# Attention units with score rounds by key tile, one value product for two heads and two query sets, and row sums added by GpSimd

## The reference

```python
def layer(x, q_w, k_w, v_w, o_w, q_b, k_b, v_b, o_b, w_gate_up, w_down):   # x: 2 x 1024 x 512
    x = x + layernorm(attn(layernorm(x)))
    x = x + layernorm(ffn(layernorm(x)))
    return x

def attn(h):                       # 16 heads of 32
    q, k, v = h @ q_w.T + q_b, h @ k_w.T + k_b, h @ v_w.T + v_b
    scores = einsum('bhqd,bhkd->bhqk', q, k) / sqrt(32)
    scores = where(ki > qi, -inf, scores)          # causal
    return einsum('bhqk,bhkd->bhqd', softmax(scores), v) @ o_w.T + o_b

def ffn(h):                        # 512 -> 2 x 2048 -> 512
    gate, up = split(h @ w_gate_up.T)
    return (silu(gate) * up) @ w_down.T
```

## Time and profile before

| | |
|---|---|
| Median of three runs (lowest, highest) | 1198.62 us (1198.29, 1202.72) |
| Span of the profiled execution | 1201.2 us; the page gives no time around it |
| Mean granted TensorE clock | 0.975 of full speed |
| Busy over the span: PE, DVE, ACT, POOL | 95%, 61%, 37%, 29% |
| Chain that ended last | PE 84%, DVE 10% |
| First T, first output matmul of batch 1 | 85.5 us, 599.1 us |

### The profile page before, as it was taken

The page is one execution under the profiler, slowest core; times in us unless marked ns, Lnnn a source line. Parts: engine busy times, 40 slices in busy tenths (PEclk is TensorE's granted clock), DMA queues, the critical chain, the costliest instruction groups (busy, mean ns, idle before and its releaser), DMA issues.

```text
span 1201.2 us, 17984 instructions
## 1 busy us (share of the span) xinstructions
PE 1137.4 (95%) x5888; PEld 784.8 (65%) x5888; DVE 729.2 (61%) x1431; ACT 446.7 (37%) x811; POOL 350.0 (29%) x205
## 2 busy tenths in 40 slices
PE   3889999999999999999997999989999899989996
PEld 2664555555575555554476888878888688868885
DVE  6674667677777766677586454564446454564444
ACT  3214555555414555555523222322223222232221
POOL 5000000000422000003044544534544444534541
PEclk9988999999999999999897999999999999999999
DMA  5312222222312222222223222243233332243230
GB/s 201 88 44 59 59 69 61 61 61 64 94 62 72 63 62 61 61 61 53 80 88 123 81 103 102 82 149 104 79 105 114 116 102 102 81 149 105 79 122 36
DMA packets 51305, 103.85 MB, mean 86 GB/s; under 512 B 9792, under 2 KB 9792, under 8 KB 51008
## 3 DMA queue, kind: packets, MB, share of 16 engines
q1 hardware_dynamic: 51264, 103.33, 28.0%
HBM read 69.74 MB, written 8.39 MB: 65 GB/s over the span
## 4 chain that ended last, share of the span: by engine, by line
PE 84%; DVE 10%; issue 2%; DMA 1%; ACT 1%; SPq 1%; POOL 0%; DVEq 0%; POOLq 0%; ACTq 0%
PE ps L975 18%; PE ps L977 17%; PE ps L976 17%; PE ps L1072 13%; PE ps L1055 10%; PE ps L1029 6%; PE ps L1058 2%; PE ps L1040 1%; DVE outs_sums L737 1%; DMA x_in<-x 1%; DVE h_lo L848 1%; DVE stats L947 1%; DVE acc L954 1%; DVE ps L775 1%; DVE xt_lo L751 1%
## 5 line engine op out<-in xcount | busy, mean ns | idle before, releaser
L478 POOL TENSOR_TENSOR gu_lo<-gu_raw,gu_hi 128x1024 fp32r<-128x1024 f32 x64 | 154.5, 2415 | 322.3 <-ACT gu_hi L657 322.3
L577 ACT ACTIVATE probs<-ps 128x512 f32<-128x512 f32 (+3 forms) x384 | 169.4, 488 | 139.9 <-PE ps L1058 97.0
L977 PE MATMUL ps<-xt_hi,gu_lo 128*128 128x512 f32 x512 | 204.3, 399 | 0.0
L976 PE MATMUL ps<-xt_lo,gu_hi 128*128 128x512 f32 x512 | 203.2, 397 | 0.0
L975 PE MATMUL ps<-xt_hi,gu_hi 128*128 128x512 f32 x512 | 203.0, 397 | 0.0
L842 DVE TENSOR_TENSOR h<-ps,silu 128x512 f32<-128x512 f32 x64 | 44.2, 691 | 258.6 <-PE ps L977 258.6
L775 DVE CUSTOM_DVE_ANT_0 ps<-ps,mask_q 128x128 f32<-128x128 f32 (+7 forms) x256 | 191.3, 756 | 0.0
L1072 PE MATMUL ps<-probs,v_pair 128*32 128x512 f32 (+3 forms) x768 | 161.4, 506 | 0.0
L1072 PE MATMUL ps<-probs,ones 128*32 128x512 f32 (+3 forms) x768 | 161.3, 506 | 0.0
L848 DVE TENSOR_TENSOR h_lo<-h,h_hi 128x512 fp32r<-128x512 f32 x64 | 159.7, 2496 | 2.2
L1055 PEld LDWEIGHTS ps<-q_stack,k_stack 98*128 98x128 f32 x384 | 70.8, 195 | 127.2 <-ACT probs L577 76.5
(11 more groups left out here) (101 smaller groups left out, 1590.4 us busy)
## 6 DMA issues: line engine op xcount, KB each, us to landing
gu_raw<-gu_w SPq DMA_DIRECT2D x64, 512.0 KB, 3.6
dn_raw<-dn_w SPq DMA_DIRECT2D x64, 256.0 KB, 2.7
x_in<-x SPq DMA_DIRECT2D x32, 256.0 KB, 3.4
q_stack<-st_hi SPq DMA_DIRECT2D x128, 64.0 KB, 2.0
k_stack<-st_hi SPq DMA_DIRECT2D x128, 64.0 KB, 2.0
qk_raw<-qk_w SPq DMA_DIRECT2D x16, 256.5 KB, 2.8
q_stack<-st_lo SPq DMA_DIRECT2D x64, 64.0 KB, 2.0
k_stack<-st_lo SPq DMA_DIRECT2D x64, 64.0 KB, 2.0
```

Source lines behind the costliest of these rows:

```text
L478: nc.gpsimd.tensor_tensor(gu_lo[:, s], gu_raw[:, s], gu_hi[:, s].bitcast(F32), ALU.subtract).then_inc(gu_split, 1)
L577: nc.scalar.activation(probs[:, j % 2, h, 0:CH - off], ps[:, ST_BANK + h, 0:CH - off], ACT.Exp, scale=SCALE).then_inc(p_ready, 1)
L976: nc.tensor.matmul(dst, hi, r_lo, start=False, stop=False)
L977: return nc.tensor.matmul(dst, lo, r_hi, start=False, stop=stop)
```

## The change

1. **Rounds.** The 1024 queries are two sets, the even tiles (half 0) and the odd tiles (half 1) of 128, 512 columns each. For a key tile kt only the tiles from the diagonal on are left. Key tiles 0 to 3 make two rounds each, one a set; 4 to 6 one round with both sets side by side in a bank; 7 one round: 12 rounds (`ROUNDS`). One exp reads both heads' banks in one instruction, and `scores(g, r)` waits for the exp of round r - 1 (`p_ready`).
2. **Values.** Eight products, one for each key tile. The four column groups hold (set 0, head 0), (set 0, head 1), (set 1, head 0), (set 1, head 1), all into one accumulator bank.
3. **Row sums.** The exps of rounds 0 and 1 are written to `p_sum`; those of rounds 2 to 11 to a ring of three (two of them in `x_in`, one `p_own`), from which GpSimd adds them to `p_sum` (`add_up`, 13 instructions). In the next unit one product with `ones` (`total`) gives the sums, in the banks of the ring.
4. **Banks.** The bank of the second accumulator takes both projection chunks. `copy_acc` is one copy, the copies of the maxima's rows are one on each engine side by side, and `waited` and `v_pair` go.
5. **Order.** TensorE's `body` is written out anew; T of unit g stands at the head of its own unit. The loops over units are unrolled. `normalise` takes its reciprocal in PSUM; for the last unit of a batch it works in two halves. The DMAs of the stacks wait for rounds 7 and 11 (`score_full`).

```diff
+ROUNDS = [(kt, (half,)) for kt in range(TT // 2) for half in range(SETS)] + [(kt, (0, 1)) for kt in range(TT // 2, TT - 1)] + [(TT - 1, (1,))]
+P_SLOTS = 3
...
+            def add_up(g, n):
+
+                kt, halves = ADDS[n]
+                r, at_col, w = PART[kt, halves[0]]
+                pool.wait_ge(p_ready, NR * g + r + 1)
...
+                slot = p_ring[ring_slot(g, r)]
+                if len(halves) == 1:
+                    total = p_sum[:, g % 2, halves[0], :, HALF - w:HALF]
+                    part = slot[:, :, 0:w]
+                    nc.gpsimd.tensor_tensor(total, total, part, ALU.add).then_inc(p_added, 1)
...
+            def exps(g, r):
+
+                act.wait_ge(score_full, NR * g + r + 1)
...
+                    before = ring_before(g, r)
+                    if before is not None:
+                        act.wait_ge(p_used, TT * before[0] + ROUNDS[before[1]][0] + 1)
+                        act.wait_ge(p_added, NADD * before[0] + before[1] - SETS + 1)
+                    to = p_ring[ring_slot(g, r)]
+                nc.scalar.activation(to[:, :, 0:WIDTH[r]], ps[:, ST_BANK:ST_BANK + 2, 0:WIDTH[r]], ACT.Exp, scale=SCALE).then_inc(p_ready, 1)
...
-                nc.vector.scalar_tensor_tensor(m_cols[:, :, 0:2, 1], m_full[:, :, :], -1.0, m_cols[:, :, 0:2, 0].bitcast(F32),
-                                               ALU.mult, ALU.subtract).then_inc(m_ready, 1)
+                nc.vector.scalar_tensor_tensor(m_lo, m_full[:, :, :], -1.0, m_hi.bitcast(F32), ALU.mult, ALU.subtract).then_inc(m_ready, 1)
...
+                if g or r:
+                    pe.wait_ge(p_ready, NR * g + r)
                 for h in range(2):
...
-                for n in range(4):
-                    lhs = v_pair[:, s, kt, n * HD:(n + 1) * HD] if n < 2 else ones[:, :]
-                    last = nc.tensor.matmul(ps[n * HD:(n + 1) * HD, ACC_BANK + c, off:CH], lhs, probs[:, j % 2, n % 2, 0:CH - off],
-                                            start=kt == 0, stop=j == CHUNK_END[c])
+                    r, at_col, w = PART[kt, half]
+                    p = p_sum[:, g % 2, r] if r < SETS else p_ring[ring_slot(g, r)]
+                    for h in range(2):
+                        rows = slice((half * 2 + h) * HD, (half * 2 + h + 1) * HD)
+                        last = nc.tensor.matmul(ps[rows, ACC_BANK, HALF - w:HALF], v[:, kt, (u * 2 + h) * HD:(u * 2 + h + 1) * HD],
+                                                p[:, h, at_col:at_col + w], start=kt == 0, stop=kt == TT - SETS + half)
...
+            def total(g):
+
+                use = use_of_sums(g)
+                bank = ring(use)
+                pe.wait_ge(p_added, NADD * (g + 1))
+                for half in range(SETS):
+                    for h in range(2):
+                        rows = slice((half * 2 + h) * HD, (half * 2 + h + 1) * HD)
+                        last = nc.tensor.matmul(bank[rows, :], ones[:, :], p_sum[:, g % 2, half, h, :], start=True, stop=True)
+                last.then_inc(bank_full, 2)
...
+                project_next(0, 0)
+                transpose_maxima(g)
+                project_next(0, 1)
+                maxima_of_next(0, 1)
+                scores(g, 0)
+                maxima_of_next(2, 3)
+                project_next(0, 2)
+                scores(g, 1)
...
+                scores(g, 10)
+                values(g, 5)
+                maxima_of_next(14)
+                scores(g, 11)
+                maxima_of_next(15)
+                values(g, 6)
+                values(g, 7)
```

## The result

| | before | after |
|---|---|---|
| Median of 11 runs each (lowest, highest) | 1200.05 us (1196.99, 1206.05) | 1207.40 us (1203.71, 1210.10) |
| Ratio after to before, 95% interval | | 1.0060 (1.0045 to 1.0075) |
| Span of the profiled execution, mean clock | 1201.2 us, 0.975 | 1204.7 us, 0.961 |
| First T, first output matmul of batch 1 | 85.5, 599.1 us | 89.0, 602.0 us |

The interval excludes 1: the kernel is slower. Its lower end, 0.45%, is still within the 0.5% that the forecast called no change. The forecast was 1191 us.

A forecast was written before the change was run, and what follows sets the result against it. TensorE was taken as the bound (busy 29.00 of 29.00 us). Savings in the units less dearer ends summed to -7.5 us from 1201.2, so 1193.7, and 1191 us with the median 2.6 lower; range 1172 to 1211 (8 in 10).

The forecast's parts named there:

- the ends: Units 14 and 15 and what follows: -0.3 us, then +11.9 us from late GpSimd adds and half clock.
- Unit 14: -0.3: Next-to-last attention unit: forecast to take 0.3 us less than before.
- 2 us within the unit: Unit 15: allowance of 2 us for half clock inside it, with 2 us more behind it.
- The negation: VectorE's second small operation ahead of the maxima's transposes, held by a GpSimd add: 0.1 us, bounded by 0.7.
- The middle: Eighth to tenth transposes of the maxima, across the first output projection: 109.1 us for 110.75, so -1.7.
- The product itself: Value product with four different streams overlaps: 8 steps, 0.99 us each at 512 columns, saving 3.0 us a unit.
- The hand-off: Between rounds, the next score waits for the exp of both heads: 1.97 us start to start at 512 columns.
- The unit: Steady attention unit, from one transposing of the maxima to the next: 27.5 us, bounds 26.3 and 29.0.
- Start and unit 0: Kernel start: first transposes of the maxima 1.3 us later; unit 0 then 2.5 us shorter.
- The forecast case: Whole kernel: 27.5 us a unit and 1191 us, own range 1184 to 1199; chance 0.46.
- the hand-offs and the tail cost what the products saved: Rival: rounds 0.1 us dearer, negation held by adds; 29.0 us a unit, ends +12, total 1210; chance 0.17.
- the three signs: Wrong if a unit is under 26.8 or over 28.5 us, each unit's exp awaits GpSimd, or end costs under 5.

The follow-up runs named there:

- e1: Changed kernel plus 16 groups of three TensorE matmuls whose result nobody reads, in units 14 and 15; 1201.7 us, ratio 1.001 to the kernel before.
- e10: e8 plus the unread matmuls of e1 and twelve more such groups around the last sums and behind the last; 1177.9 us, ratio 0.9817 to the kernel before.
- e8: e2 with one exp per head and round in place of one for both heads; 1183.8 us, ratio 0.9863 to the kernel before.
- e2: Changed kernel with GpSimd's adds of rounds 10 and 11 deferred behind the next unit's negated maxima, except in a batch's last unit; 1199.9 us, ratio 1.0004.
- e6: e2 and e1 together, with unit 15's row sums made by TensorE in place of GpSimd's adds; 1194.1 us, ratio 0.9953 to the kernel before.
- e4: Changed kernel with each GpSimd add cut to 2 columns a head, so row sums are incomplete; 1203.8 us, ratio 1.0038 to the kernel before.
- e3: Changed kernel with GpSimd's attn splits in each batch's last two units waiting for the unit's first exp; ratio 1.0059 to the kernel before.

## Why the forecast was wrong

**The step that failed is the ends**, "Unit 14: -0.3" and the last unit with its "2 us within the unit". They were to cost 11.6 us together and cost 17.9: 6.3 more, the largest miss in the sum. The forecast took units 14 and 15 at full clock but for 2 + 2 us, on the strength of the earlier trace rows, where the kernel before lost it for one piece of 7 us. It had worked out that nothing fills the hand-offs there and that TensorE would be idle for 8 us, and allowed no more than that for what it does to the clock. The changed kernel ran 37 us there at 1.2 GHz. e1 (some 6 us back with more work) and e10 against e8 (2.4 + 2.7 us) show it. The mechanism behind the wait at the end was right: with the clock kept, TensorE waits for the last add, which ends 27.0 us after T (e1) for 25.7 forecast.

**The negation, 0.1 us, was 0.41.** In steady units the bound of 0.7 held, the value did not: the forecast looked at the second of the two operations, which reads two operands of SBUF, and passed over the first, which reads one. The first one is held. Over 13 units that makes most of the 4.6 us missed there. Without it (e2) the ratio is 1.0004: level with the kernel before, not under it. With the fill as well, and the sums of the last unit on TensorE (e6), it is 0.9953. The rule of the Trainium skill (SBUF — State Buffer, Who interferes with whom) that the forecast cited names this case too: a `tensor_scalar` can enter a mode that takes both ports, and whoever comes second waits for the whole instruction. The 0.59 and 1.93 us, each ending with GpSimd's instruction, agree with it.

**The middle, -1.7, was +1.2.** The first output matmul came 37.5 us after T (35.3 forecast): the last add of unit 7 ended 28.4 us after T, 1 us later than worked out, TensorE waited for it, and the sums ran at half clock:

```profile
312.62 1.93 PE L1155 MATMUL ps<-p_sum,ones 128*32 128x512 f32 x8 [2.65 <-POOL p_sum L542]
```

**Right, by the runs.** The product itself: a 512-column value step with four different streams costs 0.99 us from start to next start (235.21 to 236.20), as did one with `ones` in it; it overlaps. The hand-off: 2.02 us for 1.97. The unit: 27.47 for 27.5, once the negation is free. GpSimd's adds: 1.83, 1.28 and 0.72 us, and no ring wait that cost anything in steady units (e4). T to the first score 2.52 for 2.35. Busy time of a stretch of 29 us after, for the earlier trace rows: TensorE 27.2 of 29.0 us, ScalarE lower, GpSimd up from 1.8 to 18.8 us.

```profile
149.00:178.00 29.00, 27.16 (x176) 16.79 (x175) 21.00 (x43) 13.74 (x20) 18.84 (x14) 1.00 0.25 63
```

**Not settled.** Start and unit 0: together -4.0 for -1.2. Before, half clock stands at 76 to 87 and at 93 to 104 us; after, at 73 to 77 and 80 to 87. Where these pieces fall differs between kernels that are alike there (unit 0 took 27.9 us in the changed kernel, 29.0 in e2, 29.3 in e3), so unit 0 of a single profile is partly luck, and why the clock falls where it does there was not tested.

**What the time alone would say.** "The forecast case" and the rival "the hand-offs and the tail cost what the products saved" differ by the unit (27.5 or 29.0). The time, 1207.4 us, came out near the rival's 1210, and the unit, 27.87, near the forecast's. None of the three signs that the forecast named for being wrong appeared: the unit is between 26.8 and 28.5 us, no exp is held up by GpSimd in each unit, and the end costs over 5 us. The time alone would have confirmed the wrong story, and the signs would have confirmed the forecast, since none of them set an upper limit on the ends.

## What to carry to other kernels

Merging two small instructions of the next engine (one exp for two heads) saves that engine time it may not need, and makes the first consumer wait for the last producer: ScalarE had 13 us to spare, and 24 exps in place of 12 were 0.7 us a unit faster. A small operation on the critical path should not share its moment with a long GpSimd instruction; moving GpSimd's work behind it cost nothing in the steady units. Where a change thins out TensorE's work, price the stretch at half clock first, and look at the last iterations of a pipeline, where the filling work has run out.

## What was not expected of the hardware

- A VectorE operation on 16 elements a partition with a single SBUF operand, 0.18 us by itself, takes 0.59 us behind a GpSimd add of 0.72, and 1.93 behind a subtraction of 2.34 us. The two-operand one was held too: 0.95 us beside a cast of 1.04 (at 534.90).
- Adding work shortened the kernel: 16 groups of three matmuls nobody reads took some 6 us off (e1); in e10 unit 14 gained 2.4 us by 8 of them.
- The maxima on VectorE, which read PSUM and one operand of SBUF, hardly moved with GpSimd adding beside them: 1.25 us on average at 1024 columns, for 1.22 before.
